# A mixture-of-experts stage on one core: one row group of the shared expert moves from ahead of the expert loop into it, and the groups in the loop stand every fourth expert instead of every fifth

## What is computed

```python
X = x.reshape(-1, D)                       # 4096 tokens, D = 256, after the layer norm
logits = (X @ gate_w.T)
scores = sigmoid(logits)                   # 32 experts
_, idx = top_k(scores + bias, 4)           # four experts for each token
w = take_along_axis(scores, idx); w = w / sum(w)
pos = place of the token in its expert's queue; valid = pos < C      # C = 256 rows an expert
xe[expert, pos] = X[token]                 # routed rows
h = silu(xe @ W1) * (xe @ W3)              # each expert: 256 -> 128
ye = h @ W2                                # 128 -> 256
out[token] = sum over its experts of w * ye[expert, pos]
out = out + silu(X @ sw1.T) * (X @ sw3.T) @ sw2.T                    # the shared expert, all tokens
x = x + out
```

## Time and profile before

| | |
|---|---|
| median of three runs | 2179.09 us (2174.68 to 2187.6) |
| the profiled execution's own time | 2180.86 us |
| its span in the profile | 2179.1 us |
| granted TensorE clock over the span | 0.937 of full |
| busy over the span: PE / DVE / ACT / POOL | 88% / 62% / 50% / 54% |
| last stage, from the end of the attention | about 1934 us to 2179 us |
| POOL's 64 adds of expert rows (L987) | 2016.47 us to 2141.2 us |

### The profile page before, as it was taken

How to read it: one execution, slowest core, us unless ns; L and a number is a source line. 1 busy time by engine, 2 the same in 40 slices (tenths; PEclk the granted TensorE clock), 3 DMA queues, 4 the chain that set the end, 5 groups by cost and what they waited for, 6 DMA issues and landing times. The chain is left out here.

```text
span 2179.1 us, 39171 instructions
## 1 busy us (share of the span) xinstructions
PE 1915.9 (88%) x11815; PEld 1437.9 (66%) x11816; DVE 1360.6 (62%) x3638; ACT 1078.8 (50%) x2250; POOL 1176.0 (54%) x1159
## 2 busy tenths in 40 slices
PE   4852999999779999999999999999999999973870
PEld 2541888888666667677777777777777777752650
DVE  6765344444367777756777656777656777653763
ACT  5321333334355555646655646555646555521760
POOL 3455232323216665536587836587836587835782
PEclk8765999999889999999999999999999999986995
DMA  9762533333331212102121102121102121122979
GB/s 331 216 211 86 124 51 51 51 52 50 78 98 50 54 46 57 55 23 62 43 77 49 48 23 62 40 57 48 50 23 60 42 57 48 41 92 60 203 131 255
DMA packets 215680, 177.29 MB, mean 81 GB/s; under 512 B 85442, under 2 KB 200727, under 8 KB 214880
## 3 DMA queue, kind: packets, MB, share of 16 engines
q1 hardware_dynamic: 177904, 138.78, 22.0%
q0 software_dynamic: 28656, 27.61, 8.5%
q10 hardware_dynamic: 8960, 8.92, 1.2%
HBM read 95.05 MB, written 80.72 MB: 81 GB/s over the span
## 5 line engine op out<-in xcount | busy, mean ns | idle before, releaser
L948 POOL TENSOR_TENSOR c_den_late<-c_den_late,c_p 128x512 f32<-128x512 f32 (+3 forms) x384 | 409.7, 1067 | 239.9 <-ACT c_p L1256 196.8
L1256 ACT ACTIVATE c_p<-PS 128x512 f32<-128x512 f32 (+3 forms) x768 | 343.1, 491 | 217.0 <-PE PS L2463 126.6
L2484 PE MATMUL PS<-c_p,c_vh 128*64 128x256 f32 (+1 forms) x2816 | 319.4, 347 | 0.0
L2432 PE MATMUL PS<-c_k,c_q 128*128 128x512 f32 (+2 forms) x768 | 288.8, 376 | 11.8 <-DVE c_max L1824 5.2
L2455 PE MATMUL PS<-c_q,c_k 128*128 128x512 f32 (+2 forms) x768 | 283.3, 373 | 2.5 <-DMA c_q<-c_mr 1.8
L2484 PEld LDWEIGHTS PS<-c_p,c_vh 128*64 128x64 f32 x2816 | 202.9, 136 | 101.5 <-issue 38.2
L884 POOL DMA_INDIRECT acc<-b_y,b_tok x71 | 110.5, 1557 | 276.0 <-ACT b_y L1126 245.8
L2456 PE MATMUL PS<-c_q,c_k 128*128 128x512 f32 (+2 forms) x768 | 258.6, 348 | 0.0
L1247 ACT ACTIVATE c_q<-PS 64x512 fp32r<-64x512 f32 x256 | 151.1, 590 | 206.7 <-PE PS L2419 180.8
L1831 DVE CUSTOM_DVE_ANT_0 PS<-PS,c_maskq,c_max 128x128 f32<-128x128 f32 (+3 forms) x256 | 143.1, 559 | 116.1 <-PE PS L2432 81.3
L1824 DVE TENSOR_REDUCE c_max<-PS 128x1 f32<-128x512 f32 x256 | 174.9, 683 | 56.3 <-PE PS L2432 53.8
(11 more groups left out here) (304 smaller groups left out, 4006.0 us busy)
## 6 DMA issues: line engine op xcount, KB each, us to landing
c_vh<-c_v SPq DMA_DIRECT2D x64, 256.0 KB
c_rrow<-rden SPq DMA_DIRECT2D x63, 256.0 KB, 3.7
routed<-b_empty SPq DMA_DIRECT2D x32, 289.0 KB, 10.4
d_xe<-routed SPq DMA_DIRECT2D x32, 289.0 KB
b_xt<-routed SPq DMA_DIRECT2D x71, 130.0 KB
b_w12T<-in_w12T_dram SPq DMA_DIRECT2D x16, 512.0 KB, 14.0
d_acc<-acc SPq DMA_DIRECT2D x16, 512.0 KB, 8.9
c_st_hi<-wqk_split SPq DMA_DIRECT2D x48, 128.0 KB
```

The source lines that it names most:

```text
L948: pool.tensor_tensor(den[:, off:], den[:, off:], p, ALU.add).then_inc(s_cPa, 1)
L1256: act.activation(c_p[:, P_AT[h][m]:P_AT[h][m] + WIDTH[m]], PS[:, ST_BANK[m % STB], skip:skip + WIDTH[m]], ACT.Exp, scale=ATT_SCALE).then_i ...
L2432: pe.matmul(PS[:, 2 + use[0], 0:max(w, 256)], c_q1[h][:, t * P:(t + 1) * P], c_k1[h][:, c * 512:c * 512 + max(w, 256)], start=True, stop=T ...
L2484: ins = pe.matmul(dst, c_vh[h][:, j, :], moving, start=(j == 0), stop=(t0 == 2 + a))
```

## The change

`EARLY` goes from 3 to 2, and the step of `LATE` from 5 to 4.

```diff
-        EARLY = 3
+        EARLY = 2
 
         def shared_bank(g):
             return SHARED_BANK[g % 2] if g < EARLY else 6
 
-        LATE = {4 + 5 * n: EARLY + n for n in range(NG - EARLY)}
+        LATE = {4 + 4 * n: EARLY + n for n in range(NG - EARLY)}
```

## The result

The changed kernel took 2193.33 us in the median of five runs (2188.8 to 2196.59). The kernel before took 2175.53 over the five runs it then had (2173.83 to 2187.6). The ratio is 1.0072 with a 95% interval of 1.0055 to 1.0088: slower by 0.7%, some 15.7 us (the two medians by themselves lie 17.8 us apart). Timed ratios are of fast runs alone; one execution of before, of 3796.38 us, taken beside three of the later kernels, is left out as slow. The profiled execution of the changed kernel took 2193.02 us, with a span of 2191.2; between the two profiled executions lie 12.2 us.

A forecast was written before the change was run, and what follows sets the result against it. POOL was taken to bound the expert loop at 3.73 us an expert. Terms -2.5 + 15.7 - 6.8 + 5.1 = +11.5 us on the median 2179.09 gave 2190.6, likeliest case 2187 to 2194, 8 in 10 2181 to 2197.

The forecast's parts named there:

- The start: Head of the last stage: without group 2's second product PE's first transpose goes at 2001.6, not 2004.07; -2.5 us.
- The rival that the unexplained stalls would strike here: Expert 0's first ACT or DVE instructions: a stall makes the start's term 0 to +2.5, sum 2193 to 2196; chance 0.12.
- The steps: Expert loop: PE waits 2.9 us for DVE's adds, so four experts cost 17.97 us; five steps, +15.7 us.
- The clock: PE's waits before `shared_hidden` drop the tensor clock; three falls of 1.7 us taken of five possible, +5.1 us.
- POOL's end: From `shared_hidden` behind expert 24 to POOL's last add: 39.2 us instead of 46.0, its backlog gone; -6.8 us.
- the tail: Behind POOL's last add, to the end of the stage: fixed, the same as before.
- The rival on the other side: Expert loop: PE's wait is hidden, POOL stays the bound at 14.9 us a step; 2176.6 us (-2.5), chance 0.08.

The follow-up runs named there:

- the fill: The change plus three unneeded matmuls in PE's list ahead of each `shared_hidden` that waits: 1.0036 of the kernel before, loop 133.12 us.
- the adds-first kernel: The change with DVE's two adds of a group moved from the end of its round to the beginning: 0.9990 of the kernel before, loop 121.88 us.
- the fill of one: The change plus one unneeded matmul in PE's list ahead of each `shared_hidden` that waits: 1.0082 of the kernel before, loop 139.67 us.

## Why the prediction was right, point by point

The forecast was 2190.6 us and slower; measured were 2193.33 and a ratio of 1.0072, inside the range. How near the time came is in part luck: the median of before, from which the forecast starts, fell from 2179.09 to 2175.53 with two more runs, while the loss was +11.5 in the forecast and 15.7 timed, and the two errors partly cancel. The change is slower by over 0.5%, to which the prediction gave 0.42, and 0.55 to staying within. In the profiles the sum can be held against the rows.

**The start.** Forecast -2.5: the first transpose near 2001.6. It came at 2001.24, right behind the load's landing, in a run whose stage stood 0.4 us earlier (1996.22 for the last scatter, 1996.60 before). The chain of waits after:

```profile
1996.22 1.94 DMA routed<-r_rows,r_slot
1998.15 0.17 SPq L795
1998.33 0.04 issue
1998.37 2.35 DMA d_xe<-routed
2000.72 0.52 issue
2001.24 1.13 PE PS L2803 x4
```

So the landing came when it was forecast, allowing for the 0.4 us. But the term was taken from the wrong row. At 2004.07 before stands the load of weights, which went ahead while PE still ran the second product; the transposes themselves began at 2004.49. PE's timeline, before and after:

```profile
2004.49 1.91 PE L2803 MATMUL PS<-ident,d_xe 128*128 128x128 f32 x8
...
2001.24 1.97 PE L2803 MATMUL PS<-ident,d_xe 128*128 128x128 f32 x8 [34.75 <-DMA d_xe<-routed]
```

From transposes to transposes it is 3.25 us, less the 0.38 of the earlier stage 2.87, where 2.5 was forecast. POOL's first add won 3.05. The 0.2 between them came behind the transposes, where PE's clock rose some 0.5 us earlier against them (before near 2011.2, by a granted clock of 0.89 over 2011 to 2012; after near 2007.4, by 0.78 over 2007 to 2008). That the clock made the 0.2 is likely, not shown. The rival that the unexplained stalls would strike here didn't occur. They were still there, 7.02 us ahead of DVE's add, but ended at 1983 (DVE's timeline after):

```profile
1983.06 0.69 DVE L2118 TENSOR_TENSOR X<-PS,X 128x512 f32<-128x512 f32 x1 [7.02 <-remote]
```

What holds DVE there was not tried.

**The steps.** Forecast 17.97 us each without falls, measured 17.86 (2016.10 to 2033.96), 18.16 (2073.69 to 2091.85), the only other step that begins with a fast block, and 18.07 and 18.19 with the fill. The wait was forecast at 2.9 and is 2.95. The pattern of one step of before, taken instruction by instruction, held. That the order of the adds, and not their cost, made it is shown by the adds-first kernel.

**The clock.** Forecast three falls of 1.7, 5.1; there were four of 1.63, 6.5, in the profiled run, three in the second. Here is the term that was too small, by one fall. Three was a choice between none and five; that it came near is luck. The prediction read the waits of 1.94 us that cost nothing as the safe side, and the fill of one was expected on that ground to have few falls or none. It shows that 2.1 us isn't safe ahead of this block. The Trainium skill ("TensorE: Matmul & The Clock Gate", HAM oscillation) describes a loop with waits of about 3 to 5 us between bursts of about 2, every round of it slow. The prediction carried that over to waits of 2.9 us in a loop that is busy otherwise: of the ten blocks behind a wait in the two profiles of the change seven were slow, so neither three nor all of five.

**POOL's end.** Forecast 39.2 from the sixth block to the last add without a fall in that block; it was 2152.66 - 2111.81 = 40.85 with one, 39.2 + 1.65. The backlog was used up as forecast. The whole in the rows: -3.4 (the first `shared_hidden`, 2016.10 for 2019.53), + 21.6 (five steps, 95.7 for 74.1), - 5.1 (40.85 for 45.98) = +13.0 at the last add, where +11.5 was forecast. Without their three falls the five steps are 90.8 us for 89.9 forecast. So the start came 0.9 better and the steps 0.9 worse than forecast, which cancel, and the rest of the miss is the falls, 6.5 for 5.1. Behind the last add the tail, forecast as the same, was 0.9 us shorter (38.54 for 39.45).

**The runs.** By the profiles the change costs 12 to 13 us, timed it is 15.7 and 15.5. The profiled execution of before (2180.86) lay 5.3 us above the later median of its kernel. Which part of the stages ahead differs in such runs is open; the start of the last scatter varies by 5.4 us between profiles.

**The rival on the other side**, the wait hidden and POOL the bound, is what the adds-first kernel makes true: 14.75 to 15.07 us a step, which was the point named.

## What to carry to other kernels

When work is packed closer in hand-ordered lists, count the distance between a producer and its waiter in what each list does between them: one expert less turned a hidden chain of 3.8 us into the bound. Then look for the producer's idle time, since the cure here was the place of two adds in one list. And if the wait must stay, try unneeded matmuls in it: they kept the clock up and halved the loss.

## What was not expected of the hardware

The granted clock fell not in PE's wait but 0.4 to 1.4 us into the dense block behind it (2034.8 for a block begun at 2033.96, 2058.2 for 2056.82; so in all fourteen falls of the four kernels' profiles), and it fell for waits of 2.1 and of 2.94 to 3.23 us but never for 1.3 or 0.4, in three to four of the four or five blocks of a profile, in two profiles of the same kernel not in the same ones. A look at the clock of the wait alone would have shown 1.00 and nothing wrong. Each fall made a block of 3.70 us one of 5.40. Waits of 1.94 us elsewhere in the loop, ahead of light work, had no such effect.
